# Attention stage of a fused layer: the result stores and the row loads on another queue and at another place, the row copies one half step earlier

## The reference

```python
xn = layernorm(x)
x = x + attention(xn) + mixture_of_experts(xn)
```

## Time and profile before

| what | value |
|---|---|
| median of 3 runs | 1667.3 us (1666.17 to 1670.19) |
| the profiled execution | 1655.14 us, its span 1653.4 us |
| mean granted TensorE clock | 0.973 |
| busy over the span | PE 92%, PEld 76%, DVE 67%, ACT 59%, POOL 67% |
| third stage | about 905 to 1653 us |
| one middle turn | about 44.4 us |

### The profile page before, as it was taken

How to read it: one execution, slowest core, us unless ns; L and a number is a source line. 1 busy time by engine, 2 the same in 40 slices (tenths; PEclk the granted TensorE clock), 3 DMA queues, 4 the chain that set the end, 5 groups by cost and what they waited for, 6 DMA issues and landing times.

```text
span 1653.4 us, 38959 instructions
## 1 busy us (share of the span) xinstructions
PE 1520.1 (92%) x11382; PEld 1252.6 (76%) x11382; DVE 1105.7 (67%) x3788; ACT 979.6 (59%) x2043; POOL 1109.0 (67%) x1158
## 2 busy tenths in 40 slices
PE   4878868999999999999998899999999999999998
PEld 4766747998888999888997666677777777667766
DVE  7999875666666666666666566766666676666652
ACT  5767744454455455544554466666666666666664
POOL 1878775334433444434331488999999999999998
PEclk9999988999999999999999599999999999999999
DMA  6777755554555555545576477878877777788752
GB/s 195 269 269 269 286 195 184 170 165 156 162 165 168 160 170 164 162 138 176 164 245 149 89 155 159 178 167 174 172 173 163 163 155 164 165 168 176 168 133 88
DMA packets 228581, 288.89 MB, mean 175 GB/s; under 512 B 59488, under 2 KB 146144, under 8 KB 228512
## 3 DMA queue, kind: packets, MB, share of 16 engines
q1 hardware_dynamic: 170064, 207.30, 46.9%
q10 hardware_dynamic: 45488, 45.36, 9.6%
q0 software_dynamic: 12960, 35.41, 8.5%
HBM read 198.07 MB, written 79.95 MB: 168 GB/s over the span
## 4 chain that ended last, share of the span: by engine, by line
PE 58%; DVE 15%; ACT 10%; issue 8%; ACTq 4%; POOL 3%; DMA 2%; DVEq 0%; POOLq 0%
PE psum L152 33%; PE psum L970 11%; PE psum L1573 5%; PE psum L1531 4%; ACT plain_arena L1688 4%; PE psum L1554 2%; DVE split_arena L736 2%; PE psum L1157 2%; DVE plain_arena L1804 2%; ACTq L1707 1%; DVE stats L631 1%; ACTq L1708 1%; DVE split_arena L729 1%; ACT plain_arena L1702 1%; ACT plain_arena L1749 1%
## 5 line engine op out<-in xcount | busy, mean ns | idle before, releaser
L152 PE MATMUL psum<-split_arena 128*128 128x512 f32 (+2 forms) x4752 | 939.0, 350 | 12.3 <-DVE split_arena L1261 7.3
L152 PEld LDWEIGHTS psum<-split_arena 128*128 128x128 f32 x4752 | 750.3, 192 | 132.6 <-issue 22.9
L1804 DVE CUSTOM_DVE_ANT_0 plain_arena<-psum,mask 128x256 f32<-128x256 f32 (+1 forms) x1024 | 338.4, 385 | 198.0 <-PE psum L1531 194.2
L1688 ACT ACTIVATE plain_arena<-psum 128x512 f32<-128x512 f32 (+1 forms) x512 | 250.3, 541 | 201.7 <-PE psum L1554 171.9
L1120 POOL TENSOR_TENSOR split_arena<-plain_arena,split_arena 128x1024 fp32r<-128x1024 f32 x43 | 103.2, 2401 | 227.3 <-ACT split_arena L1192 227.0
L1226 ACT ACTIVATE plain_arena<-psum 128x512 f32<-128x512 f32 (+1 forms) x172 | 90.2, 525 | 249.7 <-PE psum L152 249.6
L970 PE MATMUL psum<-split_arena 128*128 128x256 f32 x1704 | 217.9, 286 | 3.5 <-DVE split_arena L1291 3.5
L970 PEld LDWEIGHTS psum<-split_arena 128*128 128x128 f32 x1704 | 208.0, 191 | 5.7 <-DVE split_arena L1291 4.1
L1296 DVE TENSOR_TENSOR plain_arena<-psum,plain_arena 128x512 f32<-128x512 f32 (+1 forms) x172 | 102.3, 595 | 139.9 <-ACT plain_arena L1226 137.6
L1112 POOL DMA_INDIRECT plain_arena<-xn_d,run_ix x142 | 137.1, 965 | 69.2 <-POOL run_ix L1109 35.2
L1448 POOL TENSOR_SCALAR_AFFINE_SELECT plain_arena<-plain_arena 128x1024 f32<-128x1024 f32 x128 | 140.5, 1098 | 39.5 <-ACT plain_arena L1688 38.7
(11 more groups left out here) (199 smaller groups left out, 1852.7 us busy)
## 6 DMA issues: line engine op xcount, KB each, us to landing
plain_arena<-in_gate_w SPq DMA_DIRECT2D x43, 512.0 KB, 3.4
plain_arena<-in_up_w SPq DMA_DIRECT2D x43, 512.0 KB, 4.1
plain_arena<-in_down_w SPq DMA_DIRECT2D x43, 512.0 KB, 3.4
plain_arena<-in_x SPq DMA_DIRECT2D x32, 512.0 KB, 7.0
q_d<-split_arena SPq DMA_DIRECT2D x32, 512.0 KB, 3.6
k_d<-split_arena SPq DMA_DIRECT2D x32, 512.0 KB, 5.1
split_arena<-q_d SPq DMA_DIRECT2D x128, 128.0 KB, 4.4
split_arena<-k_d SPq DMA_DIRECT2D x128, 128.0 KB, 4.8
```

Of the source, the lines that this page charges most:

```text
L152: last = pe.matmul(out, lhs_t(p), rhs(q), start=(begins and c == 0 and k == 0), stop=(ends and c == len(chunks) - 1 and k == 2), skip_grou ...
L1688: act.activation(b_pt[:, g % 2, 2 * p + par, 4 * half:4 * half + n, :].rearrange("p k s -> p (k s)"), psum[:, 2 + par, 0:n * P], ACT.Exp, ...
L1804: last = dve.tensor_tensor_reduce(b_junk[:, 2 * par + i % 2, 0:cols], psum[:, par, at:at + cols], mask[:, 2 * P - cols:2 * P], -1.0, 3e38, ...
```

## The change

Four edits in the third stage:

1. ACT no longer issues the result store. SP issues it in half step 9, behind a wait for `b_fin`, and ahead of the load of the input rows. In the last turn it is issued in two halves of 256 KB, each as soon as its half is ready.
2. SP's load of the normalised rows goes from half step 8 to half step 12, behind the loads of input rows, q, k and v.
3. `rows_hi` and `rows_lo` go from half steps 4 and 5 to 3 and 4, the ones in which PE transposes.
4. The last wait, for all stores, is SP's and no longer ACT's.

```diff
--- before.py
+++ after.py
@@ -1415,6 +1415,11 @@
                 sp.dma_start(b_zb[:, c, :], rz_d[c, :, :].unsqueeze(1).to_broadcast([2 * HG, DH, S])
                              ).then_inc(b_zbl[c], 16)
 
+            def store_half(b, half):
+                sp.wait_ge(b_fin, 2 * b + half + 1)
+                sp.dma_start(of[ds(b * S + half * HALF, HALF), :].rearrange("(a p) d -> p a d", p=P),
+                             b_o[:, 2 * half:2 * half + 2, :]).then_inc(b_st, 16)
+
             def turn(t):
                 for h in range(H):
                     b, c = due_chunk(t, h, LAG_RS)
@@ -1430,15 +1435,24 @@
                     b, g = due_group(t, h, 7)
                     if b is not None:
                         load_v(b, g)
-                    if h == 8 and valid(t):
-                        hold_after(sp, b_tr, 2 * t)
-                        sp.dma_start(b_x[:, :, :], xn_d[ds(t * S, S), :].rearrange("(a p) d -> p a d", p=P)
-                                     ).then_inc(b_ldx, 16)
+                    if h == 9 and valid(t - 2):
+                        if isinstance(t, int) and t == B + 1:
+                            for half in range(2):
+                                store_half(t - 2, half)
+                        else:
+                            hold(sp, b_fin, 2 * (t - 2) + 2)
+                            sp.dma_start(of[ds((t - 2) * S, S), :].rearrange("(a p) d -> p a d", p=P),
+                                         b_o[:, :, :]).then_inc(b_st, 16)
                     if h == 10 and valid(t - 1):
                         hold_after(sp, b_st, 16 * (t - 1))
                         sp.dma_start(b_o[:, :, :], xf[ds((t - 1) * S, S), :].rearrange("(a p) d -> p a d", p=P)
                                      ).then_inc(b_ldo, 16)
+                    if h == 12 and valid(t):
+                        hold_after(sp, b_tr, 2 * t)
+                        sp.dma_start(b_x[:, :, :], xn_d[ds(t * S, S), :].rearrange("(a p) d -> p a d", p=P)
+                                     ).then_inc(b_ldx, 16)
             turns(sp, turn)
+            sp.wait_ge(b_st, 16 * (B + 1))
 
         def b_gpsimd(pool):
             def zero_masked(b, g, p):
@@ -1772,8 +1786,8 @@
                         stage(t - 1)
                     if h == 5 and valid(t - 1):
                         stage_total(t - 1)
-                    if h in (4, 5) and valid(t - 1):
-                        rows_hi(t - 1, h - 4)
+                    if h in (3, 4) and valid(t - 1):
+                        rows_hi(t - 1, h - 3)
                     b, c = due_chunk(t, h, LAG_CH)
                     if b is not None:
                         context_hi(b, c)
@@ -1783,15 +1797,10 @@
                     for k in {0: (5, 6), 1: (7,)}.get(h, ()):
                         if valid(t - 2):
                             scale_routed(t - 2, k)
-                    if h == 9 and valid(t - 2):
-                        act.wait_ge(b_fin, 2 * (t - 2) + 2)
-                        act.dma_start(of[ds((t - 2) * S, S), :].rearrange("(a p) d -> p a d", p=P),
-                                      b_o[:, :, :]).then_inc(b_st, 16)
                     b, g = due_group(t, h, LAG_M)
                     if b is not None:
                         maxima_lo_out(b, g)
             turns(act, turn)
-            act.wait_ge(b_st, 16 * B)
 
         def b_vector(dve):
             def masked_max(b, r):
@@ -1859,8 +1868,8 @@
                     b, c = due_chunk(t, h, LAG_RC)
                     if b is not None:
                         reciprocals(b, c)
-                    if h in (4, 5) and valid(t - 1):
-                        rows_lo(t - 1, h - 4)
+                    if h in (3, 4) and valid(t - 1):
+                        rows_lo(t - 1, h - 3)
                     if h in (7, 8) and valid(t - 2):
                         finish(t - 2, h - 7)
             dve.wait_ge(b_nz, 1)
```

## The result

The changed kernel takes 1679.3 us in the median of 20 runs, the one before 1668.1 in 20 runs of its own. The ratio is 1.0063, with a 95% interval from 1.0047 to 1.008. It is slower by 0.6%, where 1662.65 us was forecast.

A forecast was written before the change was run, and what follows sets the result against it. PE and POOL were both taken as nearly full in the third stage's middle turns. +0.75 - 4.8 + 0 - 0.6 = -4.65 us on 1667.3 gave 1662.65 us; 8-in-10 range 1656.5 to 1672, the forecast's own 1659 to 1667.

The forecast's parts named there:

- Part 1: Row copies a half step earlier: PE's stall of 1.13 us a turn only moves; +0.05 a turn, +0.75 us in all.
- four links of one chain: Times from ACT's row copy through DVE's maxima to PE's values, each good to some 0.1 us; -0.3 to +0.4 a turn.
- Part 2: Store off ACT's queue: the maxima load behind it lands before half step 12 needs it, -4.8 us (bounds 0 to -7.6).
- the trace is nearer to the second: At the maxima load: engines alternate between queues, so it gets past the store, rather than shared engines keeping it waiting.
- the rival with 0.20: Queue move does nothing, since DMA engines are shared and the maxima load waits as long: 1667.5 us, chance 0.20.
- The excess of turn 2: Turn 2 over the fastest period: 2.96 us, a 1.89 wait for the maxima load and about 1.07 around it.
- Part 3: SP's queue with store and later row load: POOL's 4.8 us wait for input rows shrinks, off PE's path; counted 0.
- at 1365 and not 1366: Store on SP's queue: issued 0.8 us later than by ACT, yet expected to land at 1365 instead of 1366.
- The slower rival: Row load ahead of the reciprocal store delays the spread, so POOL waits at `normalise`: about 1674 us, chance 0.18.
- Part 4: Last store in two halves at the end: gain between 0 and 0.7 us, taken as 0.6.
- The base: Starting time of the sum: 1667.3 us, median of the runs shown, 12.2 above the profiled execution.

The follow-up runs named there:

- the first experiment: Kernel before with only the row copies `rows_hi` and `rows_lo` one half step earlier: 1672.25 against 1659.89 us, ratio 1.0075.
- the last experiment: Kernel before with only `rows_hi` early, `rows_lo` left, store on SP's queue and row load in half step 12: 1651.25 against 1658.65 us, ratio 0.9959.
- the row load's experiment: Kernel before with only the row load moved from half step 8 to 12: 1657.76 against 1659.89 us, ratio 0.9979.

## Why the prediction was wrong, point by point

**Part 1, PE's chain: right.** The stall was to move to the scores of half step 5 and keep its size, with +0.05 us a turn. It is there in both kernels that have the copies early:

```profile
1092.50 0.94 PE L1545 MATMUL psum<-split_arena 48*128 48x256 f32 x3 [0.68 <-DVE plain_arena L1813]
```

The waits at the maxima transpose and the values are gone, and the good turns are 0.1 us longer, well within the -0.3 to +0.4 of the text.

**Part 1, what else stands behind `rows_lo`: the step that failed.** The text said "What changes is what stands behind them", and then followed PE's waits alone. In DVE's list `reciprocals` of half step 5 stands behind `masked_max` too. The copies made it 0.35 us later against the values (-0.50 to -0.15). Its result goes out by a small DMA in SP's queue, and SP stands still until that has landed. The reverse experiment, which swapped these reciprocals with the copy behind them and nothing else, cost 0.6%, and the order that puts them first took the loss away in both kernels. So that this operation's lateness sets off the loss is shown. The bounds of -4.5 to +6 us for part 1 were made of errors in four links of one chain. The second chain was not in them: it costs 12.4 us by the medians of the first experiment (8.4 by the profiled third stages, 766.5 and 758.1).

The path from there is read from the traces, and each link was not tried by itself. With the row load in half step 8 it is the one that the first experiment shows: the spread's 256 KB start later, the DMA engines are full behind it, and the maxima load lands too late for half step 12. In before it was on time in most turns with little to spare, and that margin the prediction did not look at.

With the row load in half step 12, behind the store on SP's queue, the waits come later. In the turns 6, 8, 9, 11 and 13 of after the first chunk's gap is 2.5 to 2.8 us, and in these the second chunk's is 5.15 to 5.73. In the turns 3, 4, 5, 7, 10 and 12 the first is 1.9 to 2.1 and the second 2.6 to 3.9. The same second gap is 3.1 to 4.0 with the copies back. From turn 3 on, the waits at half steps 0 and 4 stand in the five turns of the first kind, and in turn 14. A late first spread is the usual way into such a turn and not the only one: in turn 14 the first gap is 2.08 and the second 5.06, and the long turn of the last experiment has 1.89 and 6.12. The turns 7 and 10 are 45.8 and 45.2 us long without such a wait. In turn 7 PE waits 0.95 us for `masked_max` at half step 8, right behind the long sixth turn; turn 10 was not explained.

**Part 2, the store off ACT's queue: the term of -4.8 us measured 0** (0.9996, with the gain at the end in it). The step that failed is "the trace is nearer to the second", the choice between two rules. I took the fact that waits stand only behind the store for an effect of the queue. It is one of traffic: in those half steps the row load, the q and k loads and the store are under way together, and taking the row load out gave what changing the store's queue did not. By the Trainium skill (Trainium Kernel Development and Optimization, Key Constraints) transfers of all queues share 16 engines and another issuer saves only issue time. The trace agrees, with 1.78 us of wait in turn 2 for 1.89. That was the rival with 0.20. The excess of turn 2, of which the prediction could name 1.89 of 2.96 us, is in part the clock: from 1011 to 1014 us, around that wait, the granted clock of before was 0.56.

**Part 3, SP's queue: counted 0.** The row load gains where it stands now: 0.9979 alone. (It had 11 half steps of cover and not 15; the 7 that it keeps are right.) The store's move, counted 0 here, costs in company: 1.0063 for 1.0003. The store does not land earlier, as I had expected ("at 1365 and not 1366"). From its issue to the input load it takes 6.57 us in the sixth turn, and POOL waits 12.0 us for the input rows in six turns, where it was 4.8 in one:

```profile
POOL plain_arena L1497 <- DMA plain_arena<-in_x: 12.0, 6, 2.8
...
POOL plain_arena L1472 <- DMA plain_arena<-rz_d: 4.5, 6, 1.5
```

**The slower rival: right place, wrong condition.** Its place was the row load ahead of the reciprocal store, and in after the spread is late there, and POOL waits for it (second row above). But that its price came through POOL is not shown: the long turns have PE's waits for maxima and k loads. And with the copies back the same order is a gain. In most of the bad turns a late first spread had come before.

**Part 4, the end: right, as far as one trace of each shows.** From the start of the last `finish` to the end it was 4.1 us and is 3.3, a gain of 0.8 where 0.6 was taken. From the last issue to the end it was 3.4 and is 2.6 (3.0 and 2.4 in the text). One trace of each is compared, and no run tried the two halves alone:

```profile
1649.31 0.69 DVE L1843 TENSOR_TENSOR plain_arena<-psum,plain_arena 128x512 f32<-128x512 f32 x1 [0.74 <-PE psum L152]
```
```profile
1676.01 0.69 DVE L1852 TENSOR_TENSOR plain_arena<-psum,plain_arena 128x512 f32<-128x512 f32 x1 [0.74 <-PE psum L152]
```

**The base.** 1667.3 us stood for the kernel before, and its 20 runs have 1668.1, so the base took no part in the error. Put together from the single runs the sum is: part 1 +12.4, part 2 with the end 0, the row load -2.1. That gives +10.3 us where 11.1 were measured, and the agreement is luck. The parts do not add: copies and row load together give 1.0003 and not 1.0054, and the store's move then brings the 0.6%.

## What to carry to other kernels

When an operation moves in a fixed order, list everything behind it on its engine, and follow above all what ends in a DMA, when the stretch behind it has its DMA engines full. An issue that is on time says little there: ask when the transfer can start and what must move behind it. Here 0.35 us on DVE became 12 us in the first experiment, while the stall on the critical engine that everybody looks at stayed where the sum had it. And before giving a DMA another queue, ask whether it waits for its queue or for the traffic: moving another large load away from the tight stretch tells the two apart. A move that is neutral in one kernel can cost 0.6% in company, as the store's did here, so the combinations have to be run.

## What the runs showed of the hardware that I had not expected

**A 16 KB store has steps in its time.** From the issue of the first chunk's reciprocals to the release of the spread it is either 1.85 to 1.87 us or 2.77 to 2.84 in the turns 3 to 14 of the first experiment. In the row load's experiment it is 1.85 to 1.87 in all of them. In other orders there are values between and above (2.5 to 2.6 with the reciprocals behind the copy, 2.1 to 3.1 with them first). Right behind the 512 KB row load the second chunk's is 5.06 to 6.12 in the bad turns. Why there are two values is open. The Trainium skill (DMA: Bandwidth & Descriptors, Latency and other measured facts) puts most of a small transfer's fixed cost into the receipt of the write in HBM, and says that it grows with the load on HBM. The traces agree in direction, with 1.86 us in most turns of before and 5.42 behind the row load in the sixth of after, but no run here varied HBM's load alone.

**A wait of PE can cost more than itself.** In the first experiment it is so in turn 6 (above). After the wait of 1.83 us in the sixth turn of after, the granted clock was 0.76 and 0.67 in the next 6 us, and full again behind them:

```profile
1224.00:1227.00 3.00, 0.60 (x4) 1.00 1.03 155
1227.00:1230.00 3.00, 2.84 (x19) 0.76 1.07 147
1230.00:1233.00 3.00, 3.00 (x24) 0.67 0.37 79
1233.00:1240.00 7.00, 5.85 (x68) 1.00 0.44 109
```

Between 1.2 and 2.4 GHz, its two levels, 0.67 is a stretch with both in it. In before the wait of 0.97 us in turn 6 left the clock at 1.00. It is not the length alone: in after, 1.14 us at 1319.80 was followed by 0.62 (1320 to 1323), and 1.49 us at 1458.17 by 1.00 (1458 to 1461).

**Untouched stages scatter more than this change moves.** The first two stages took 895 to 910 us in the profiled executions, and the kernel before has medians from 1658.65 to 1670.91 on different chips. Only ratios on one chip, and the third stage by itself, could be compared.
